# Shared units of a mixture stage: from straight-line code to a loop on TensorE, with second buffers, their own weight home and four raw slots

## The reference, cut to what matters

```python
def _L1_ffn_ref(x, gate_w, w1, w2, w3, ws1, ws2, ws3):   # x: normalised tokens, 4096 x 256
    weights, indices = _gate(xt, gate_w)                  # softmax over 16 experts, 2 groups of 4, top 4
    c = c.at[jnp.arange(T)[:, None], indices].add(weights)
    h1 = jnp.einsum('td,edi->tei', xt, w1)
    h3 = jnp.einsum('td,edi->tei', xt, w3)
    a = jax.nn.silu(h1) * h3
    y = jnp.einsum('tei,eid,te->td', a, w2, c)
    z = jax.nn.silu(xt @ ws1) * (xt @ ws3) @ ws2          # the shared part, 256 wide: two units of 128
    return y + z                                          # x = x + 0.5 * this
```

## Time and profile before

| | |
|---|---|
| three runs | 4229.5, 4232.49, 4232.69 us; median 4232.49 |
| profiled execution's own time | 4239.63 us |
| its span | 4237.8 us, mean granted TensorE clock 0.886 |
| busy | PE 3424.7 us (81%), PEld 2593.1, DVE 2384.6, ACT 2002.2, POOL 1201.3 |
| stage d | from about 1895 to 2407 us; its shared units from 2274 to 2403 |
| stage f | from about 3621 to the end; its shared units from 3999 to the end |

### The profile page before, as it was taken

How to read it: one execution, slowest core, us unless ns; L and a number is a source line. 1 busy time by engine, 2 the same in 40 slices (tenths; PEclk the granted TensorE clock), 3 DMA queues, 4 the chain that set the end, 5 groups by cost and what they waited for, 6 DMA issues and landing times. The chain is left out here.

```text
span 4237.8 us, 71259 instructions
## 1 busy us (share of the span) xinstructions
PE 3424.7 (81%) x23666; PEld 2593.1 (61%) x23669; DVE 2384.6 (56%) x4824; ACT 2002.2 (47%) x4064; POOL 1201.3 (28%) x1030
## 2 busy tenths in 40 slices
PE   4599948989896389973798699999999999369833
PEld 4499935555555279962797556566656665358832
DVE  4644446656664644437555375666576565565544
ACT  1566624444452356645443265655565565344410
POOL 2154321212112035422553021122112200235545
PEclk6699978999997589985898799999999999679966
DMA  3243220000003044333355300011001000424533
GB/s 123 92 109 87 34 62 6 16 27 16 19 14 114 22 132 109 68 54 116 129 163 141 109 26 26 7 31 32 15 18 31 28 5 6 152 83 162 163 116 112
DMA packets 209017, 293.85 MB, mean 69 GB/s; under 512 B 32992, under 2 KB 170208, under 8 KB 208480
## 3 DMA queue, kind: packets, MB, share of 16 engines
q1 hardware_dynamic: 155744, 176.32, 12.6%
q0 software_dynamic: 52992, 113.82, 11.5%
HBM read 193.20 MB, written 96.86 MB: 68 GB/s over the span
## 5 line engine op out<-in xcount | busy, mean ns | idle before, releaser
L2441 ACT ACTIVATE e_prob<-e_s_ps,e_small 128x512 f32<-128x512 f32 x512 | 346.9, 684 | 172.4 <-PE e_t_ps L2331 94.1
L2577 DVE TENSOR_REDUCE e_small<-e_s_ps 128x2 f32<-128x1024 f32 x256 | 313.2, 1224 | 148.9 <-PE e_s_ps L2318 142.1
L1849 ACT ACTIVATE b_pt<-b_t_ps 128x1024 f32<-128x1024 f32 (+3 forms) x256 | 180.9, 706 | 306.6 <-PE b_t_ps L1781 305.6
L2532 POOL TENSOR_TENSOR e_wide<-e_small,const 128x512 f32<-128x512 f32 x64 | 66.6, 1041 | 779.0 <-DVE e_small L2666 779.0
L2331 PE MATMUL e_t_ps<-const,e_prob 128*128 128x128 f32 x2048 | 270.6, 274 | 13.6 <-ACT e_pt L2430 8.1
L2352 PE MATMUL e_z_ps<-e_pt,e_v 128*64 128x512 f32 x1024 | 275.5, 617 | 0.4 <-DVE e_zf L2673 0.4
L2331 PEld LDWEIGHTS e_t_ps<-const,e_prob 128*128 128x128 f32 x2048 | 235.1, 141 | 61.4 <-issue 22.3
L2032 DVE TENSOR_REDUCE b_small<-b_s_ps 128x2 f32<-128x1024 f32 (+3 forms) x256 | 209.8, 819 | 82.3 <-PE b_s_ps L1760 78.3
L2583 DVE COPY e_pt<-e_t_ps 128x512 f32<-128x512 f32 x256 | 175.6, 686 | 69.0 <-PE e_t_ps L2331 65.3
L692 DVE TENSOR_TENSOR ce_h_lo<-ce_hid,ce_h_hi 128x512 fp32r<-128x512 f32 x128 | 88.7, 693 | 206.9 <-ACT ce_h_hi L639 179.4
L692 DVE TENSOR_TENSOR ae_h_lo<-ae_hid,ae_h_hi 128x512 fp32r<-128x512 f32 x128 | 88.7, 693 | 205.9 <-ACT ae_h_hi L639 179.7
(11 more groups left out here) (743 smaller groups left out, 11240.9 us busy)
## 6 DMA issues: line engine op xcount, KB each, us to landing
o_rows_dram<-d_big SPq DMA_DIRECT2D x36, 512.0 KB
o_rows_dram<-f_big SPq DMA_DIRECT2D x36, 512.0 KB
ae_raw<-w_dram SPq DMA_DIRECT2D x16, 1024.0 KB
ce_raw<-w_dram SPq DMA_DIRECT2D x16, 1024.0 KB
d_big<-x_dram SPq DMA_DIRECT2D x16, 512.0 KB, 9.1
f_big<-x_dram SPq DMA_DIRECT2D x16, 512.0 KB, 8.7
d_raw<-m_dram SPq DMA_DIRECT2D x54, 128.0 KB, 3.5
f_raw<-m_dram SPq DMA_DIRECT2D x54, 128.0 KB, 3.6
```

Of the source, the lines that this page charges most:

```text
L1849: act.activation(pt[:, kt % 2, a, :, 0:width], t_ps[:, :, 0:width], ACT.Exp).then_inc(p_ready, 1)
L2441: act.activation(prob[:, at], s_ps[:, at], ACT.Exp, bias=nmx[:, at:at + 1], accum_out=sums[:, buf, h * QT + s:h * QT + s + 1]).then_inc(p_ ...
L2577: dve.tensor_reduce(nmx[:, at:at + 2], s_ps[:, at:at + 2], AX.X, ALU.max, negate=True).then_inc(mx_ready, 1)
```

## The change

In both mixture stages:

- `RAW` is 4 instead of 6.
- The shared units' weights get a home of their own, `zw_hi` and `zw_lo`; `takes` begins at the start of `w_hi`. The small tiles are packed in pieces of 512 words instead of 1024.
- ACT splits the two shared units in steps 4 and 5 of the expert steps, DVE makes their low parts in steps 6 and 7, and the four `factor` parts in steps 2 to 5.
- A second buffer for the hidden high and low parts, in `w_lo`, used by odd groups.
- On TensorE the shared units are a hardware loop of three turns with two groups a turn: turn, down, turn, down, up, up; before it turn 0, turn 1, up 0, up 1, after it the last two downs.
- `collect` is divided into `own_part` and `collect`; a semaphore `po_free`, begun by a small memset after the steps, says when `po` may be written. DVE does both own parts of a pair, with the next splits between, then the collects.

```diff
-RAW, TAKE, BY_POOL = 6, 8, 12
+RAW, TAKE, BY_POOL = 4, 8, 12
...
-            def z_down(g):
-                pe.wait_ge(zh_lo, (g + 1) * SHARED)
-                if g:
-                    pe.wait_ge(zo_used, g)
+            def z_down(g, b):
+                pe.wait_ge(zh_lo, g * SHARED + SHARED)
+                pe.wait_ge(po_free, g + 1)
...
-            z_turn(0)
+            for b in range(2):
+                z_turn(b, b, 0)
             pe.wait_ge(*lo_done(E1 + SHARED - 1))
-            z_up(0)
-            z_turn(1)
-            pe.wait_ge(y_act, TILE_STEPS)
-            pe.wait_ge(y_dve, TILE_STEPS)
-            for g in range(NG):
-                if g + 1 < NG:
-                    z_up(g + 1)
-                if g + 2 < NG:
-                    z_turn(g + 2)
-                z_down(g)
+            for b in range(2):
+                z_up(b, b)
+            with pe.Fori(0, NG // 2 - 1) as i:
+                for b in range(2):
+                    z_turn(i * 2 + (b + 2), b, i + 1)
+                    z_down(i * 2 + b, b)
+                for b in range(2):
+                    z_up(i * 2 + (b + 2), b)
+            for b in range(2):
+                z_down(NG - 2 + b, b)
...
 ACT, in step j:
+                if isinstance(j, int) and 4 <= j < 4 + SHARED:
+                    split_w(E1 + j - 4)
...
-            for u in range(E1, E1 + SHARED):
-                split_w(u)
-            z_turned(0)
+            for g in range(2):
+                z_turned(g)
             for g in range(NG):
                 z_silu(g, 0)
-                if g + 1 < NG:
-                    z_turned(g + 1)
                 z_high(g, 0)
                 z_silu(g, 1)
+                if g % 2 and g + 1 < NG:
+                    z_turned(g + 1)
                 z_high(g, 1)
+                if g % 2 and g + 1 < NG:
+                    z_turned(g + 2)
...
 DVE, in step j:
+                if isinstance(j, int) and 2 <= j < 2 + TOPK:
+                    factor(j - 2)
+                if isinstance(j, int) and 6 <= j < 6 + SHARED:
+                    low(E1 + j - 6)
...
-            for u in range(E1, E1 + SHARED):
-                low(u)
-            for k in range(KC):
-                split(0, k, zx_hi, pa, zx_lo)
+            dve.wait_ge(y_act, TILE_STEPS)
+            dve.memset(r1[:, 0:1], 0.0).then_inc(po_free, 1)
+            dve.wait_ge(factored, 1)
+            for g in range(2):
+                for k in range(KC):
+                    split(g, k, zx_hi, pa, zx_lo)
             for g in range(NG):
                 z_mult(g, 0)
-                if g + 1 < NG:
-                    split(g + 1, 0, zx_hi, pa, zx_lo)
                 z_low(g, 0)
-                if g < 2:
-                    factor(2 * g)
                 z_mult(g, 1)
-                if g + 1 < NG:
-                    split(g + 1, 1, zx_hi, pa, zx_lo)
+                if g % 2 and g + 1 < NG:
+                    for k in range(KC):
+                        split(g + 1, k, zx_hi, pa, zx_lo)
                 z_low(g, 1)
-                if g < 2:
-                    factor(2 * g + 1)
-                if g:
-                    collect(g - 1)
-            collect(NG - 1)
+                if g % 2:
+                    own_part(g - 1)
+                    if g + 1 < NG:
+                        for k in range(KC):
+                            split(g + 2, k, zx_hi, pa, zx_lo)
+                    own_part(g)
+                    for each_g in (g - 1, g):
+                        if each_g < here:
+                            collect(each_g)
```

More of the change, by code:

```diff
@@ L1061, in z_down @@
                         cols = slice(t * P, (t + 1) * P)
-                        last = mm3(pe, out, z_half(hh)[:, n, cols], z_half(hl)[:, n, cols], w_hi[:, c:c + D], w_lo[:, c:c + D],
+                        last = mm3(pe, out, z_hh[b][:, n, cols], z_hl[b][:, n, cols], zw_hi[:, c:c + D], zw_lo[:, c:c + D],
                                    n == 0, n == SHARED - 1)
@@ L1113, in split_w @@
                 act.wait_ge(w_in[u % RAW], 48 * (u // RAW + 1))
-                copy(expert_w(w_hi, u % E1), raw[:, u % RAW], w_hi_done)
+                if u >= E1:
+                    act.wait_ge(*lo_done(E1 - 1))
+                copy(expert_w(w_hi, u) if u < E1 else expert_w(zw_hi, u - E1), raw[:, u % RAW], w_hi_done)
             def norm(g):
@@ L1171, in z_high @@
                 act.wait_ge(zhid_ready, g * SHARED + n + 1)
-                if g:
-                    act.wait_ge(zo_ready, g)
-                copy(z_half(hh)[:, n], hid[:], zh_hi)
+                if g >= 2:
+                    act.wait_ge(zo_ready, g - 1)
+                copy(z_hh[g % 2][:, n], hid[:], zh_hi)
             def hot_rows():
@@ L1424, in z_low, with own_part @@
                 dve.wait_ge(zh_hi, g * SHARED + n + 1)
[L1425 to L1427 removed]
+                dve.tensor_tensor(z_hl[g % 2][:, n], hid[:], z_hh[g % 2][:, n].bitcast(F32), ALU.subtract).then_inc(zh_lo, 1)
+            def own_part(g):
                 dve.wait_ge(zo_ready, g + 1)
@@ L1433, in collect @@
                     last = dve.scalar_tensor_tensor(xr[:, g % 2, t], part, 0.5, xr[:, g % 2, t], ALU.mult, ALU.add)
-                last.then_inc(zo_used, 1)
-                if g >= here:
-                    return
-                dve.wait_ge(zo_used, g + 1)
-                if g == 0:
-                    dve.wait_ge(factored, 1)
+                last.then_inc(po_free, 1)
+            def collect(g):
+                dve.wait_ge(po_free, g + 2)
                 for k in range(TOPK):
```

44 lines of the change are left out of this document (22 added, 22 removed).

## The result

The changed kernel takes 4219.95 us, median of 11 runs (4211.85 to 4223.55), the kernel before 4230.81 (4217.04 to 4236.41), both measured in turn on one chip. The ratio is 0.9975, 95% interval 0.9966 to 0.9984. So it is faster, by 0.25%, some 11 us where 67 were forecast, and outside the range of 4146 to 4210. The profiled execution spans 4219.3 us, that of before 4237.8: 18.5 us less, more than the medians' 11, since the profiled execution of before was 7.1 us above its median (4239.63 against 4232.49) and that of the changed kernel 1.3 above (4221.2 against 4219.95).

A forecast was written before the change was run, and what follows sets the result against it. Bounds: in d TensorE's chain waits and lost clock, in f code reading beside gather bursts. -36 - 47 + 2 x (2.6 + 5) = -67.8 us gave 4171.8 profiled, 4165 against the median; range 4146 to 4210.

The forecast's parts named there:

- Shared units in d, -36: Stage d's shared units: turns of two groups take 20.0 us instead of 28.0; -36 us, bounds -25 and -42.
- its price for collect 0: Start of d's shared units: collect 0 ahead of group 2's product costs 8 us, with the clock lost by it.
- Shared units in f, -47: Stage f's shared units: one hold of TensorE stays, near the first pass's end; -47 us, bounds -60 and 0.
- the remark that in stage f the trace disagrees with hidden crossings of code blocks: Stage f: reading TensorE's new code beside a burst of gathers stalls some 25 us each time, four times.
- a hold in every turn: Rival: jumping back reads code again, or bursts themselves hold; f stays as it is, d's gain stands: 4212, chance 0.10.
- The ideal of -59.7: Stage f's shared units if nothing holds TensorE: POOL's 128 gathers of 1.26 us, 161.3 us, are the bound; -59.7 us.
- Routing, +2.6 a stage: Routing, twice: with four slots late loads land later, and table load and exponential follow; +2.6 us a stage, 0 to 6.
- the ring would be a chain: Rival, routing: four slots make loads wait on each other, once a unit's wait exceeds about 4.9 us; 4237 or more, chance 0.05.
- Expert steps, +5 a stage: Expert steps, twice: factor 0 adds 3.3 us before step 3's low part, other factors and low parts 1.7; +5 a stage.
- f's term at 0: Stage f's shared units: the upper bound, no gain, of the -47 us term.

The follow-up runs named there:

- e3: Changed kernel with one 128x256 memset on GpSimd, and a wait for it, after each gather of the collects: 4198.47 us, 0.9882 of before.
- e8: Changed kernel with a pause of two 128x256 memsets and their waits after each four gathers of the collects: 4168.34 us, 0.9855 of before.
- e11: e8 with slots for the rows of twelve tiles in place of eight (TAKE = 12): 0.9833 of before.
- e12: e8 with VectorE's collects spread over the turn as in e4: 0.9830 of before.
- e5: Kernel before, with one 128x256 memset and a wait after each gather of the collects: 4217.57 us, 0.9973 of before.
- e9: Kernel before, with two 128x256 memsets and their waits after each four gathers of the collects: 4206.93 us, 0.9909 of before.
- e2: Changed kernel with TensorE's loop over turns of two groups written out straight, in the same order: 4233.48 us, 0.9965 of before.
- e1: Changed kernel without the collects' gathers and VectorE's waits for them (added rows left out): 4107.99 us, one run, 0.966 of before.
- e14: Kernel before without the collects' gathers and the waits for them (added rows left out): 4141.84 us, one run, 0.975 of before.
- e4: Changed kernel with the odd group's collect put off to the middle of the next turn, gathers unpaced: 4221.46 us, 0.9939 of before.

## Why the prediction was wrong, step by step

**Shared units in d, -36: right, -31.3.** Turns of 19.4 us for 20.0, full clock, one collect behind the first turn. What was mis-sized is the start, by its price for collect 0: 8 us were taken for landing and clock, while group 0's own part came after 6.64 us of idle time and the collect ran 15 us later than thought. Part of this is the holds' doing: with paced gathers D is 91 to 92 in the new order (e3, e8, e11, e12) and 126 in the old (e5, e9).

**Shared units in f, -47: wrong, +12.4; this is the step that failed.** It said that a hold is the reading of TensorE's new code beside a burst, so that the loop, with half the packets, would leave one hold of four. The coincidence of three packets with three bursts was taken for a cause. The runs show in its place that the gathers hold the releases by themselves when they come 1.26 to 1.4 us apart: no packet of TensorE's code in the holds from 4024 to 4074 and from 4145 to 4195, the same holds with the loop written out (e2), none once the gathers are 1.56 us apart (e3) or gone (e1), at most 3.8 us in e8, in either order of the work (e5, e9, e14). In the kernel before, the one burst of four without a packet was held too, and the forecast passed over it. So the remark that in stage f the trace disagrees with hidden crossings of code blocks falls as well: those stalls were the gathers'. The rival "a hold in every turn", which named this cause in its last words, gave 4212 with a chance of 0.10; measured was 4219.95, since f did not stay as it was but lost 12.4 us. What the prediction held against it, that the steps' loop with gathers beside it loses only 0.78 us a turn, was no argument: GpSimd waits there some 0.95 us before every second gather (2104.40 and 2107.60 in the trace of before), so they are 1.6 us apart on average, the pace at which e3 has no hold. The Trainium skill (Runtime: NRT & Kernel Launch, Instruction fetch mechanics) has a taken branch whose target is outside the window force a fetch; this case's trace shows no packet of TensorE's code in the second and third turns of f, and the ratios no cost of the loop beside the written-out form. Whether the target was outside the window here, no run shows.

A second error lies in the same step. The ideal of -59.7, "POOL is the bound", was credited to the new order. But 32 gathers of 1.26 us are 40.3 us a pair, and the old order's 28.0 fit in that as well as the new one's. All of the credit was for the holds' going, none for the order, and the order does nothing about them. What it does in f is to put both collects at the end of a turn and behind the last hold: the turns grew by 7.3 us together and the tail by 6.1. e4 bears this out: with the collects spread the three turns take 171.4 us together, in place of 180.0 and before's 172.7, and its tail, where two collects still stand in a row behind the last hold, stays at 65.1.

**Routing, +2.6 a stage: right,** +1.6 and +1.2; over all profiles of the changed order routing of d takes 141.4 to 143.0 us, of the old order 139.9 to 141.0. In d the exponential now starts behind the table load without a gap, as forecast, with the loads awaited (ScalarE's timeline; it answers to the earlier trace rows):

```profile
1966.32 0.84 ACT L1114 ACTIVATE d_w_hi<-d_raw 128x768 fp32r<-128x768 f32 x1 [1.90 <-DMA d_raw<-m_dram]
1967.51 0.84 ACT L1114 ACTIVATE d_w_hi<-d_raw 128x768 fp32r<-128x768 f32 x1 [0.35 <-DMA d_raw<-m_dram]
1968.37 1.28 ACT L1222 ACT_TABLE_LOAD   x1
1969.66 0.63 ACT L1222 ACTIVATE d_big<-d_big 128x512 f32<-128x512 f32 x1
```

In f no table load stands there, and the exponential waits 1.06 us for VectorE (3656.23), so the forecast's mechanism shows in d alone, and f's 1.2 us are not broken down. No wait for a load reaches the 4.9 us at which the ring would be a chain: the longest is 3.83 us in f (3645.62), 1.90 in d.

**Expert steps, +5 a stage: right in kind, too large.** The profiles of before and after show -0.5 and -1.0, but at one pace the new order costs 2 to 3 us a stage (the table of steps above). Factor 0 does stand between product and low part: 4 instructions from 2057.15, and step 3's low part follows at 2060.57 without idle time. But that low part is only 1.3 us later after the first one than in the old order (15.6 us for 14.3). The next one is 3.5 us later, that of step 12 some 2 to 3 us, and the loop keeps this distance to the end. Why the low part of step 1 already comes 5.3 us after the first in place of 2.3 stays open.

**The numbers.** The profile was to lose 67.8 us and lost 18.5. Of the 49.3 between, f's shared units are 59.4 and d's 4.7; routing (2.4) and the steps (11.5) came out cheaper, and unchanged code gave 0.9. Some 6 to 7 of the steps' 11.5 are pace. Against the medians the miss is larger: they were to lose 67 us and lost 11. With f's term at 0 the forecast would have read 4212. That bound was in the term, but the range stopped at 4210, and a loss in f was not considered at all: the tail behind two collects was never costed.

## What to carry to other kernels

Where a consumer waits for "remote" while the producer's own rows show the work done, look at what else is issued in that time before reordering the work: here 128 gathers at full rate on GpSimd cost 32 us (old order) or 46 (new) against the same gathers paced, and slowing them to 1.47 us each gave more than four times what the change did (1.2% against 0.25%). A new order pays where TensorE's chain is the bound (d, -31 us) and nothing where another engine's queue is (f), so ask of each stage whether the old order already fits beside the bound. Before a coincidence (packet and burst) carries a term, look for a place with only one of the two: the fourth burst of the kernel before had no packet, and was held. And before a stage's difference of a few microseconds is read from two profiles, compare a stretch that the change doesn't touch, such as one turn of a loop.

## What the runs showed that was not expected

TensorE's releases were up to 24 us late, and in order, beside gathers that GpSimd issued 1.26 us apart, while the gathers' packets took 28% of the DMA engines' time. At 1.34 to 1.40 us VectorE still waited up to 22 us, at 1.47 own parts up to 3.8 in one run and 7.4 in others, at 1.56 as long as without gathers (0.64 and 2.10 us). Rows of 256 bytes or of 1 KB, 64 or 128 of them, made no difference to the holds, and a gather of 64 rows took 0.91 us where one of 128 took 0.96. ScalarE's releases came on time in the same stretch: its copy of 0.60 us at 4058.15 was followed by VectorE's low part at 4058.78, while TensorE's releases were 15 us late. So did VectorE's, from 4059.47 to 4059.53. Which part of the chip holds them stays open; no run here tells.
